# Another order of the calls on VectorE and GpSimd in the attention part of a one-core kernel

## The reference

```python
h = _layernorm(x) * (1 + ca) + sa
x = x + ga * attn_ref(h, ...)          # part 1: three layers
h = _layernorm(x) * (1 + cb) + sb
x = x + gb * ffn_ref(h, ...)           # part 2: two layers
# one layer of ffn_ref:
q, k, v = jnp.split(shift_token(x) @ wqkv, 3, axis=-1)     # 8 heads of 64
q, k = rotary_xpos(l2norm(q) * qs, l2norm(k) * ksc)
x = x + local_attention(q, k, v) @ wo     # window of 128: own tile and the one before
h = layernorm(shift_token(x)) * lg + lb
a, g = jnp.split(h @ w1 + b1, 2, axis=-1)
x = x + (a * gelu(g)) @ w2 + b2           # hidden width 682
```

## Time and profile before

| | us |
|---|---|
| median of 3 runs (2724.17 to 2728.64) | 2726.19 |
| the profiled execution, its own time | 2722.86 |
| its span | 2721.1 |
| PE busy (share of the span) | 2611.0 (96%) |
| VectorE busy | 2179.1 (80%) |
| ScalarE busy | 1516.3 (56%) |
| GpSimd busy | 1434.8 (53%) |
| mean granted clock of TensorE | 0.989 of full |

### The profile page before, as it was taken

The page is one execution under the profiler, slowest core; times in us unless marked ns, Lnnn a source line. Parts: engine busy times, 40 slices in busy tenths (PEclk is TensorE's granted clock), DMA queues, the critical chain, the costliest instruction groups (busy, mean ns, idle before and its releaser), DMA issues.

```text
span 2721.1 us, 61573 instructions
## 1 busy us (share of the span) xinstructions
PE 2611.0 (96%) x21416; PEld 2144.9 (79%) x21416; DVE 2179.1 (80%) x5242; ACT 1516.3 (56%) x3109; POOL 1434.8 (53%) x1406
## 2 busy tenths in 40 slices
PE   6799999999999999999888999999999999999998
PEld 4588888888888888888766788888878788888877
DVE  5778877786777787888998888888888888888875
ACT  3454455445544554455246767667666667666661
POOL 2334434443433354344566766665575666676653
PEclk9999999999999999999999999999999999999999
DMA  3100000010000010000111000000011100010001
GB/s 102 28 9 9 17 2 17 9 38 2 1 2 13 13 38 9 17 25 25 50 36 54 27 14 17 10 17 14 29 33 30 30 25 22 29 32 30 19 26 44
DMA packets 77731, 65.63 MB, mean 24 GB/s; under 512 B 15394, under 2 KB 72698, under 8 KB 77434
## 3 DMA queue, kind: packets, MB, share of 16 engines
q1 hardware_dynamic: 77434, 61.70, 7.7%
HBM read 49.10 MB, written 12.58 MB: 23 GB/s over the span
## 4 chain that ended last, share of the span: by engine, by line
PE 85%; DVE 6%; issue 4%; POOL 3%; ACT 2%; DMA 1%; SPq 0%; DVEq 0%; POOLq 0%; ACTq 0%
PE PS L273 76%; PE PS L813 3%; PE PS L766 1%; PE PS L775 1%; PE PS L486 1%; PE PS L424 1%; PE PS L476 1%; PE PS L843 1%; DVE PS L1915 1%; DMA PX<-in_L_attn_x 0%; DVE PT L1931 0%; POOL SM L2443 0%; PE PS L873 0%; ACT PR L1335 0%; DVE SQ L1895 0%
## 5 line engine op out<-in xcount | busy, mean ns | idle before, releaser
L1335 ACT ACTIVATE PR<-PS,SM 128x256 f32<-128x256 f32 (+1 forms) x512 | 279.5, 555 | 102.9 <-DVE SM L1920 101.4
L1133 ACT ACTIVATE FB<-PS,BC 128x512 f32<-128x512 f32 x192 | 133.7, 696 | 315.1 <-PE PS L273 158.9
L1682 DVE TENSOR_TENSOR U<-PS,CST 128x512 f32<-128x512 f32 x384 | 238.4, 683 | 45.2 <-PE PS L273 44.9
L2309 POOL TENSOR_TENSOR RL<-FB,RH 128x512 fp32r<-128x512 f32 x96 | 125.1, 1303 | 241.7 <-DVE RH L1660 241.7
L1915 DVE CUSTOM_DVE_ANT_0 PS<-PS,MSK 128x256 f32<-128x256 f32 (+1 forms) x512 | 202.8, 437 | 44.3 <-PE PS L273 43.0
L273 PE MATMUL PS<-W2H,RH 128*128 128x256 f32 x768 | 227.8, 297 | 0.2 <-DVE RL L1663 0.2
L2443 POOL TENSOR_TENSOR SM<-SM,COL 128x8 f32<-128x8 f32 x128 | 215.3, 1682 | 10.7
L273 PE MATMUL PS<-W2H,RL 128*128 128x256 f32 x768 | 216.1, 281 | 0.0
L273 PE MATMUL PS<-W2L,RH 128*128 128x256 f32 x768 | 216.0, 281 | 0.0
L2321 POOL TENSOR_TENSOR SBD<-SBD,TMP 128x256 f32<-128x256 f32 x84 | 64.4, 766 | 217.6 <-DVE TMP L1674 217.6
L273 PE MATMUL PS<-X1H,W1H 128*128 128x512 f32 x384 | 160.9, 419 | 9.8 <-ACT FB L1133 7.9
(11 more groups left out here) (264 smaller groups left out, 8821.0 us busy)
## 6 DMA issues: line engine op xcount, KB each, us to landing
PX<-in_L_attn_x SPq DMA_DIRECT2D x16, 512.0 KB, 4.1
TB<-in_k_rot SPq DMA_DIRECT2D x64, 128.0 KB, 2.1
SG<-in_L_attn_W SPq DMA_DIRECT2D x24, 256.0 KB, 2.7
xp_scratch<-PX SPq DMA_DIRECT2D x8, 512.0 KB, 2.9
xs_scratch<-X SPq DMA_DIRECT2D x64, 64.0 KB, 1.5
ZS<-xs_scratch SPq DMA_DIRECT2D x16, 256.0 KB, 2.9
GG<-xp_scratch SPq DMA_DIRECT2D x7, 512.0 KB, 3.9
out<-GG SPq DMA_DIRECT2D x7, 512.0 KB, 5.2
```

Source lines behind the costliest of these rows:

```text
L1133: e.activation(FB[:, hb % 2, :], PS[:, 5, :], ACT.Relu, bias=BC[:, l % 2, 4 + hb:5 + hb]).then_inc(*a_re.up(n, hb))
L1335: t = e.activation(PR[:, par, 256 * i + lo:256 * i + hi], PS[:, 3 + par, 256 * i + lo:256 * i + hi], ACT.Exp, bias=S[:, 40 + 2 * g + i:41 ...
L1682: e.tensor_tensor(heads(U[:, u % 6, :], 4), heads(PS[:, g, :], 4), bcast(CM, 4), ALU.mult).then_inc(*d_mk.up(n, u))
L2309: e.tensor_tensor(RL[:, r, :], FB[:, 0, :], RH[:, r, :].bitcast(F), ALU.subtract).then_inc(*p_rl.up(n, hb))
```

## The change

VectorE's and GpSimd's loops over tiles are written anew, PE's, ScalarE's and SyncE's are kept. Where one pass was a tile, a pass is now four tiles, `for v in range(1, 15)` with u = 4v and q = v - 2; tiles 1 to 3 are written out ahead of it and tiles 60 to 63 behind it. The calls are the same, with the same semaphores; the calls of each kind stand in the same order among themselves, apart from the two halves (q and k) of `rotate`, which change places in three tiles of four, and the order among the kinds is another. The first instruction that stands elsewhere ran at 1400 us on VectorE and at 1406 us on GpSimd. The heart of the diff:

```diff
-        for u in range(1, NU):
-            i, q = u % 4, u // 4 - 2
+        for v in range(1, 15):
+            u, q = 4 * v, v - 2
...
+            inverse_sums(u - 1)
+            add_y(q - 1)
+            copy_p(u - 1, 1)
+            norm_apply(q)
...
             mixed(u - 1)
-            if u == 1:
-                rounded(23, 6)
+            reduce(u + 1, 1)
+            reduce(u + 1, 0)
             largest(u, 1)
+            low_h(q)
             largest(u, 0)
...
+            gated(q, 5)
+            largest(u + 1, 2)
+            gated(q, 2)
+            norm_centre(q + 1)
+            high_hidden(q, 2)
...
+            low_hidden(q, 1)
+            inverse_sums(u + 1)
+            gated(q, 3)
+            copy_p(u + 1, 1)
...
+            if v == 7:
+                split(P2 + 14)
...
+            mixed(u + 2)
+            largest(u + 3, 1)
+            reduce(u + 4, 1)
+            largest(u + 3, 0)
+            reduce(u + 4, 0)
+            low_x(u + 6)
```

On GpSimd one pass reads:

```diff
-        for u in range(1, NU):
-            i, q = u % 4, u // 4 - 2
+        for v in range(1, 15):
+            u, q = 4 * v, v - 2
+            inverse(u - 1, 0)
...
+            table(u)
+            low_hidden2(q - 1, 4)
+            rotate(u, 0)
+            rotate(u, 1)
+            low_o(u - 2)
+            inverse(u, 1)
+            norm_k(u)
+            table(u + 1)
...
+            inverse(u, 0)
...
+            rotate(u + 1, 0)
+            low_o(u - 1)
+            rotate(u + 1, 1)
+            inverse(u + 1, 1)
+            norm_k(u + 1)
+            inverse(u + 1, 0)
+            table(u + 2)
...
+            finish(q - 1)
...
+            rotate(u + 2, 0)
...
+            low_o(u)
+            rotate(u + 2, 1)
+            inverse(u + 2, 1)
+            norm_k(u + 2)
+            norm_rsqrt(q + 1)
+            low_hidden2(q, 0)
...
```

More of the change, by code:

```diff
@@ L2116, in _ @@
         reduce(2, 0)
-        for u in range(1, NU):
-            i, q = u % 4, u // 4 - 2
+        rounded(23, 6)
+        mixed(0)
+        split(P2 + 4)
+        largest(1, 1)
+        largest(1, 0)
+        cosine(2, 0)
+        cosine(2, 1)
+        rotated(2, 1)
+        copy_p(1, 0)
+        low_x(4)
+        rounded(23, 7)
+        add_o(0)
+        rotated(2, 0)
+        largest(1, 3)
+        norm3_b(22)
+        largest(1, 2)
+        add_down(23)
+        inverse_sums(1)
+        copy_p(1, 1)
@@ new lines, in _ @@
+        norm2_a(23)
+        mixed(1)
+        largest(2, 1)
+        reduce(3, 1)
+        largest(2, 0)
+        reduce(3, 0)
+        cosine(3, 0)
+        cosine(3, 1)
+        copy_p(2, 0)
+        rotated(3, 1)
+        low_x(5)
+        add_o(1)
+        rotated(3, 0)
+        largest(2, 3)
+        largest(2, 2)
+        norm2_b(23)
+        inverse_sums(2)
+        copy_p(2, 1)
+        norm3_a(23)
+        mixed(2)
+        largest(3, 1)
+        reduce(4, 1)
+        largest(3, 0)
+        reduce(4, 0)
@@ new lines, in _ @@
+            copy_p(u + 1, 1)
+            if v == 7:
+                split(P2 + 12)
+                split(P2 + 13)
+            mixed(u + 1)
+            largest(u + 2, 1)
+            reduce(u + 3, 1)
+            largest(u + 2, 0)
+            reduce(u + 3, 0)
+            high_hidden(q, 3)
+            cosine(u + 3, 0)
+            cosine(u + 3, 1)
+            copy_p(u + 2, 0)
+            rotated(u + 3, 1)
+            low_x(u + 5)
+            add_o(u + 1)
+            rotated(u + 3, 0)
@@ new lines, in _ @@
+            largest(u + 2, 3)
+            largest(u + 2, 2)
+            high_hidden(q, 5)
+            low_hidden(q, 5)
+            if v == 1:
+                split(P2 + 8)
+            low_hidden(q, 3)
+            inverse_sums(u + 2)
+            gated(q, 4)
+            copy_p(u + 2, 1)
+            if v == 7:
+                split(P2 + 14)
+            if v == 9:
+                split(P2 + 18)
+            high_hidden(q, 4)
+            if v == 9:
+                split(P2 + 19)
+            mixed(u + 2)
@@ new lines, in _ @@
+        low_h(13)
+        largest(60, 0)
+        cosine(61, 0)
+        cosine(61, 1)
+        add_o(59)
+        copy_p(60, 0)
+        low_x(63)
+        rotated(61, 1)
+        rotated(61, 0)
+        largest(60, 3)
+        largest(60, 2)
+        copy_p(60, 1)
+        inverse_sums(60)
+        gated(13, 0)
+        norm_stats(14)
+        high_hidden(13, 0)
+        mixed(60)
+        reduce(62, 1)
+        largest(61, 1)
+        reduce(62, 0)
+        largest(61, 0)
+        gated(13, 1)
@@ new lines, in _ @@
+        cosine(62, 0)
+        cosine(62, 1)
+        rotated(62, 1)
+        high_hidden(13, 1)
+        copy_p(61, 0)
+        add_o(60)
+        rotated(62, 0)
+        largest(61, 3)
+        gated(13, 5)
+        largest(61, 2)
+        gated(13, 2)
+        norm_centre(14)
+        high_hidden(13, 2)
+        low_hidden(13, 1)
+        inverse_sums(61)
+        gated(13, 3)
+        copy_p(61, 1)
+        mixed(61)
+        largest(62, 1)
+        reduce(63, 1)
+        largest(62, 0)
+        reduce(63, 0)
@@ new lines, in _ @@
+        high_hidden(13, 3)
+        cosine(63, 0)
+        cosine(63, 1)
+        copy_p(62, 0)
+        rotated(63, 1)
+        add_o(61)
+        rotated(63, 0)
+        largest(62, 3)
+        largest(62, 2)
+        high_hidden(13, 5)
+        low_hidden(13, 5)
+        low_hidden(13, 3)
+        inverse_sums(62)
+        gated(13, 4)
+        copy_p(62, 1)
+        high_hidden(13, 4)
+        mixed(62)
+        largest(63, 1)
+        largest(63, 0)
+        copy_p(63, 0)
+        add_o(62)
@@ L2223, in _ @@
+        largest(63, 3)
+        largest(63, 2)
+        inverse_sums(63)
+        add_y(13)
+        copy_p(63, 1)
+        norm_apply(14)
         mixed(63)
@@ L2527, in _ @@
         low_hidden(23, 6)
[L2528 to L2567 removed]
+        rotate(2, 0)
```

272 lines of the change are left out of this document (149 added, 123 removed).

## The result

The changed kernel takes 2732.82 us (median of 17 runs, 2727.25 to 2746.8) and the kernel before, on the same chips, 2724.8 (17 runs, 2716.36 to 2733.07). The ratio is 1.0039, with a 95% interval of 1.0028 to 1.0050: slower by 0.39%, some 10.6 us (the two medians themselves lie 8.0 apart), where 21 were forecast. The direction was right, the size was twice too large.

What follows compares the result with a forecast made beforehand. PE was taken to bound the kernel (85% of the chain). Terms 31 + 3.6 + 3.5 - 8.8 - 4 - 4.5 - 1 = +19.8, taken as +21, gave 2744, plus 3.3 for the median 2747 us; range 2714 to 2774.

Steps and rivals of the forecast that it cites:

- early tiles: First tiles, a ring without slack where lateness is paid in full: two passes at 1.7 more each, +3.5 us, bounds -10 to +10.
- `out_proj` waiting for OTL: Tile 4v + 3: GpSimd's rotation of q ahead of the low half makes PE wait 1.1 us a pass.
- The exponentials of tile 4v: Tile 4v: two reductions and `low_h` ahead make the exponentials 0.45 us late for PE's transposes.
- the sums of tile 4v + 1: Tile 4v + 1: `inverse_sums` behind `norm_centre` delays ScalarE's copy that `spread_sums` needs, 0.5 us a pass.
- the wait before has moved PE by as much, and I count it at nothing: Tile 4v + 3, `turn_k`: rotated k 0.9 to 1.1 us late, covered by the OTL wait, so counted as zero.
- Batch's first tiles: Tiles 16, 32, 48, half as wide: PE comes sooner to the transposes, 1.2 us more each, 3.6 in all.
- Tile 30: Weight split moved from ahead of q's rotation to behind `copy_p(30, 1)`: PE's 4.08 us wait goes, -4.5 with its aftermath.
- Tiles 36 to 43: Weight blocks spread otherwise in tiles 38 to 40: some 4.9 us gained and 3.9 lost, -1.
- Rival 1: Slack covers the lateness in the passes, only the recovery stays: -18 us, 2708; chance 0.14.
- Rival 2: Half the lateness, 1.3 us a pass or 18, balances 18 recovered: 2726, about no change; chance 0.17.
- Rival 3: Backlog: VectorE catches up too slowly, each pass costs 4.5 to 5 us, +51, 2777; chance 0.17 together with rival 4.
- Rival 4: Clock: waits bring PE to 1.2 GHz, 1.5 us a pass, 21 more, 2768; chance 0.17 together with rival 3.

## Why the prediction was right and wrong

**The sign, and the place, right.** The change was forecast slower, by lateness that PE sees, with recovered stalls against it. All of that is in the traces. The forecast failed in the size of its terms: the steady pass (33.5 us for the passes behind tile 7 with the batches' first tiles, where some 28.5 came), what is recovered (18.3, where some 22.9 came) and, the other way, the early tiles (4.6 ahead of tile 8, where 8.5 to 9.9 came). The 1.2 us that took the sum from 19.8 to 21 had no row behind them.

**A steady pass: forecast +2.3, measured +2.0**, but by other terms. The first, `out_proj` waiting for OTL, was forecast at 1.1 and measured at 0.85, with OTL ending where the sum put it (four rotations, then 1.27). The exponentials of tile 4v (0.45) and the sums of tile 4v + 1 (0.5) show no wait: 0.95 a pass too much, and the first step that failed. Those two were worked out against PE's starts of before, and PE now stands 0.85 and 0.46 later when it comes there, which would cover both (argued, no run separates it); a slack read in one trace is not the slack behind an earlier new wait. I had used just that argument for `turn_k`, and there it went too far: 0.46 and 0.32 are left where I had counted nothing and 0.25. The step that failed there is "the wait before has moved PE by as much, and I count it at nothing": I had the rotation of k 1.8 to 2 us later on VectorE, by two reductions and `low_x`, and it came 2.5 later, since PT's copy stands ahead of it too. The rest of the 2.0, some 0.4 us, is in no wait of the list.

**Batch's first tiles: forecast +3.5 for such a pass, measured +2.85** (76.95 to 79.80). Near enough, and a guess.

**Early tiles: forecast +3.5 on top of half a pass, measured +8.5 to +9.9** in three profiles of this order. The failing step is "two passes at 1.7 more each". Nearly 6 us are more idle time of PE, and the other 2.6 to 4.0 are busy time on the same work, behind waits at which the granted clock fell: the sum had no term for the clock there. The experiments took 1.6 to 5.0 us off by single edits, and how much of that is lateness and how much is the clock of one execution they don't tell apart. This part of the cause stays open.

**Recovered: the second layer right** (1.73 forecast, 1.65 measured; at the end 4 and 3.4). **Tile 30: -4.5 forecast; measured -5.6** (the pass goes from 87.2 to 83.6 against 2.0 of lateness). **Tiles 36 to 43: forecast -1**, too small: the two passes go from 85.9 + 81.4 to 83.5 + 82.2, 1.6 less in all, though they pay 4 of lateness and get 1.7 back from `finish`, so the other places of splits 17 to 23 are worth 4 against this profile of before, and more against the others above. The failing step is "some 4.9 gained and 3.9 lost by the same reckoning", for which no row was given. **The last pass** goes from 80.4 to 75.6, 4.8 less, where the sum had 4 less and, if a pass of lateness is counted there too, 1.7 less; with `finish` and `norm_apply` moved alone it lost 3.4.

From tile 8 on the sum had +15.2, and the traces show +5.6 (1127.2 to 1132.8 us from `mixed(7)` to `mixed(63)`); the runs show +1.0 for tiles 12 on. Ahead of it the sum had +4.6 and the traces +9.9; the runs of the early kernel, whose new order goes to tile 11, show +10.3. So the forecast was too high by the recovered splits and the steady rate, and too low by the early tiles, and the first error was the larger.

**Rivals.** Rival 1 (the slack covers the lateness) is out: the waits are there. Rival 2, half the lateness against what is recovered, is near the runs from tile 12 on (+1.0), but not by its own way, since the rate is 2.0 and not 1.3 a pass, and not in the whole. Rival 3 is out: a pass costs 2.0 and not 4.5 more, and VectorE's busy time fell by 63 us. Rival 4 is seen in the early tiles, where PE is busy 2.6 to 4.0 us longer, and not in the steady part, where the granted clock stayed at 1.00.

**From profile to median.** I took the median as 3.3 above the profiled execution. That was the distance for three runs; with 17 it is 1.9, and the changed kernel's was 8.75 the other way.

## What to carry to other kernels

When calls are moved on engines that feed a full TensorE, the price is set at two or three calls that stand right behind a late input; find the one whose result TensorE needs first, and put every call that nothing waits for behind it. A new order is best taken apart by windows: a repeated pass tells 0.1 us in one profile, where whole runs tell 3. That holds only at full clock: where the granted clock falls behind PE's waits, as here in the early tiles and in tiles 28 to 43 of the old order, its busy time and the granted clock have to be read beside the length, or the clock of one execution is taken for the effect of an edit. And a good find in a mixed change (here `norm_apply` apart from `finish`) is worth more alone than with the rest.
